# Softmax row sums of an attention and MoE kernel: probabilities added up per block on two engines, one ones product a block, eight shared PSUM banks

## The reference

```python
x = x + _layernorm(_L0_attn_ref(_layernorm(x), wq, wk_down, wv_down, wk_up, wv_up, wo))
x = x + _layernorm(_L0_ffn_ref(_layernorm(x), gate, experts, shared, anchors))
# attention: x is (2, 1024, 128), 8 heads in 2 groups, latent width 32
scores = jnp.einsum('bqhrd,bkhd->bhrqk', q, k) * scale
scores = jnp.where(causal, scores, jnp.finfo(scores.dtype).min)
probs = jax.nn.softmax(scores, axis=-1)
y = jnp.einsum('bhrqk,bkhd->bqhrd', probs, v)
```

## Time and profile before

| | us |
|---|---|
| median of 3 runs | 416.88 |
| lowest, highest | 416.11, 418.38 |
| the profiled execution's own time | 416.28 |
| its span, from the first to the last instruction | 414.2 |
| TensorE matmuls busy | 393.9 (95%) |
| VectorE busy | 281.5 (68%) |
| GpSimd busy | 275.7 (67%) |
| ScalarE busy | 231.4 (56%) |
| mean granted TensorE clock | 0.986 |

### The profile page before, as it was taken

How to read it: one execution, slowest core, us unless ns; L and a number is a source line. 1 busy time by engine, 2 the same in 40 slices (tenths; PEclk the granted TensorE clock), 3 DMA queues, 4 the chain that set the end, 5 groups by cost and what they waited for, 6 DMA issues and landing times.

```text
span 414.2 us, 7003 instructions
## 1 busy us (share of the span) xinstructions
PE 393.9 (95%) x2168; PEld 260.5 (63%) x2168; DVE 281.5 (68%) x711; ACT 231.4 (56%) x450; POOL 275.7 (67%) x338
## 2 busy tenths in 40 slices
PE   8998999998999999999998999999999999999993
PEld 8664555553454644444556778767887788778871
DVE  5985897882857885526347776678765686557665
ACT  4555355564545466664675455865556655665643
POOL 6124867975976498473667886498963988477651
PEclk9989999998999999999999999999999999999997
DMA  7347090083230050500000000001000000000000
GB/s 215 52 108 169 16 220 13 0 196 52 40 38 3 2 77 3 71 9 2 3 0 2 1 1 2 0 0 28 1 1 2 25 2 0 1 2 25 0 2 25
DMA packets 9906, 14.56 MB, mean 35 GB/s; under 512 B 1232, under 2 KB 5520, under 8 KB 9488
## 3 DMA queue, kind: packets, MB, share of 16 engines
q1 hardware_dynamic: 9584, 13.49, 15.7%
q10 hardware_dynamic: 288, 0.64, 0.5%
HBM read 6.26 MB, written 1.05 MB: 18 GB/s over the span
## 4 chain that ended last, share of the span: by engine, by line
PE 77%; POOL 7%; DVE 6%; ACT 4%; issue 3%; DMA 2%; SPq 1%; POOLq 0%; DVEq 0%; ACTq 0%
PE ps L1240 9%; PE ps L1242 9%; PE ps L1241 9%; PE ps L1354 9%; PE ps L1333 9%; PE acc L1368 8%; PE total L1378 5%; PE acc L1439 4%; PE acc L1441 4%; PE acc L1440 4%; POOL silu L839 3%; DMA qst<-q_lo 2%; PE ps L1336 2%; PE ps L1356 1%; PE ps L1388 1%
## 5 line engine op out<-in xcount | busy, mean ns | idle before, releaser
L839 POOL TENSOR_TENSOR silu<-silu,cwb 128x512 f32<-128x512 f32 x80 | 102.5, 1292 | 40.3 <-ACT silu L971 35.8
L1095 DVE TENSOR_REDUCE nmax_h<-ps 128x1 f32<-128x512 f32 (+3 forms) x152 | 92.3, 655 | 47.8 <-PE ps L1336 24.3
L940 ACT ACTIVATE probs<-ps 128x512 f32<-128x512 f32 (+1 forms) x152 | 80.0, 579 | 70.2 <-PE ps L1354 43.7
L759 POOL TENSOR_TENSOR probs<-probs 128x768 f32<-128x768 f32 (+2 forms) x48 | 78.0, 1644 | 34.0 <-ACT probs L940 21.2
L1172 DVE TENSOR_TENSOR h_lo<-ps,h_hi 128x512 fp32r<-128x512 f32 (+1 forms) x84 | 57.0, 686 | 23.8 <-ACT h_hi L981 23.2
L1167 DVE TENSOR_TENSOR ps<-silu,ps 128x512 f32<-128x512 f32 (+1 forms) x84 | 57.9, 693 | 22.3 <-POOL silu L839 17.5
L971 ACT ACTIVATE silu<-ps 128x512 f32<-128x512 f32 x80 | 47.5, 597 | 45.5 <-PE ps L1242 39.7
L1333 PE MATMUL ps<-kst,qst 96*128 96x512 f32 (+3 forms) x192 | 63.8, 386 | 4.0 <-ACT probs L940 1.9
L1240 PE MATMUL ps<-xT_hi,w_hi 128*128 128x512 f32 x164 | 65.4, 399 | 1.3 <-ACT silu L971 1.3
L1242 PE MATMUL ps<-xT_hi,w_lo 128*128 128x512 f32 x164 | 64.4, 393 | 0.0
L1241 PE MATMUL ps<-xT_lo,w_hi 128*128 128x512 f32 x164 | 64.4, 393 | 0.0
(11 more groups left out here) (191 smaller groups left out, 518.7 us busy)
## 6 DMA issues: line engine op xcount, KB each, us to landing
qst<-q_hi SPq DMA_DIRECT2D x14, 256.0 KB, 5.6
qst<-q_lo SPq DMA_DIRECT2D x7, 256.0 KB, 6.1
x_sb<-in_attn_x SPq DMA_DIRECT2D x4, 256.0 KB, 6.5
raw<-in_ffn_w_gate SPq DMA_DIRECT2D x1, 1024.0 KB, 4.9
raw<-in_ffn_w_up SPq DMA_DIRECT2D x1, 1024.0 KB, 6.4
raw<-in_ffn_w_down SPq DMA_DIRECT2D x1, 1024.0 KB, 5.0
kst<-k_hi SPq DMA_DIRECT2D x6, 128.0 KB, 3.7
result<-x_sb SPq DMA_DIRECT2D x3, 256.0 KB, 2.3
```

The lines of the kernel that those rows point to most:

```text
L759: nc.gpsimd.tensor_tensor(into, into, probs[:, k % KTBUF, js, cols], ALU.add).then_inc(added, 1)
L839: nc.gpsimd.tensor_tensor(silu[:, k % HRING, :], silu[:, k % HRING, :], cwb[:, m % 2, t // ET, :], ALU.mult).then_inc(scaled_ready, 1)
L940: nc.scalar.activation(probs[:, k % KTBUF, j:j + w, at:at + cols], bank(full)[:, 0:w * cols].rearrange("p (w c) -> p w c", w=w), ACT.Exp). ...
L1095: nc.vector.tensor_reduce(nmax_h[:, n % 2, i, j:j + w, h], bank(full)[:, 0:w * keys].rearrange("p (w k) -> p w k", w=w), AX.X, ALU.max, ne ...
```

## The change

The sums of a block are now all gathered in the buffer of its first tile, the others being added to it one after the other. Each later tile is added by two instructions: GpSimd takes the first `SPLIT[n]` heads of block n, VectorE the rest. The split is 2 and 2 in blocks 0, 6 and 7, and 3 and 1 in blocks 1 to 5. The ones product is made once a block. The first tile's buffer stays taken until this product is made, so three buffers turn for the other tiles (`buffers()`); an `exp` waits for both adds of the tile that lay there before. `acc` and `total` are gone as named banks: `pv`, `ones`, `down`, the warming products and the tail take their banks from one pool of eight. The first `silu`, `hi` and `lo` wait only for the buffer that each lies over (`rows_left`), not for the whole second pass.

```diff
-BANKS = 6
+BANKS = 8
+ADDERS = ("POOL", "DVE")
+SPLIT = (2, 3, 3, 3, 3, 3, 2, 2)
...
+def part_heads(n, part):
+
+    return (SPLIT[n], REP) if part else (0, SPLIT[n])
...
-                if kt % 2:
-                    for half in range(2):
-                        step("POOL", ("add", n, kt, half), 2 * (8 + cols * 252 // 1000), rank - 0.1, ("pv", n, kt - 1),
-                             *[e for e in exps if half in halves_of(e)])
-                    step("PE", ("ones", n, kt - 1), 10 + (CH - first_col(n, kt - 1)) * 17 // 100, rank - 0.2, ("add", n, kt, 0), ("add", n, kt, 1),
-                     ("ones", n, kt - 3) if kt > 1 else n >= 1 and ("recip", n - 1))
+                for part, engine in enumerate(ADDERS):
+                    if kt:
+                        j, end = part_heads(n, part)
+                        cost = 18 + (end - j) * cols * 215 // 1000 if engine == "POOL" else 15 + (end - j) * cols * 105 // 1000
+                        step(engine, ("add", n, kt, part), cost, rank - 0.1, ("pv", n, 0), *[e for e in exps if part in parts_of(e)], kt > 1 and ("add", n, kt - 1, part))
+        step("PE", ("ones", n), 10 + CH * 17 // 100, n + 2.9, *(("add", n, kts(n) - 1, part) for part in range(len(ADDERS))), bank=1, until=("recip", n))
...
+                elif kind == "add":
+                    _, n, kt, part = ev
+                    j, end = part_heads(n, part)
+                    cols = slice(first_col(n, kt), CH)
+                    into = probs[:, BUF[n, 0], j:end, cols]
+                    dve.wait_ge(pv_done, PV["pv", n, 0])
+                    dve.wait_ge(exp_ready, max(EXP["exp", *e[1:]] for e in p2_steps(n) if e[2] == kt and part in parts_of(e)))
+                    if kt > 1:
+                        dve.wait_ge(added[part], ADD[part]["add", n, kt - 1, part])
+                    nc.vector.tensor_tensor(into, into, probs[:, BUF[n, kt], j:end, cols], ALU.add).then_inc(added[part], 1)
...
-                        if okt % 2:
-                            act.wait_ge(added, ADD["add", on, okt, 1])
+                        if okt == 0:
+                            act.wait_ge(ones_done, ONES["ones", on])
                         else:
-                            act.wait_ge(ones_done, ONES["ones", on, okt])
+                            for part in range(len(ADDERS)):
+                                act.wait_ge(added[part], ADD[part]["add", on, okt, part])
...
-                    if k == 0:
-                        act.wait_ge(pv_done, len(PV))
-                        act.wait_ge(ones_done, len(ONES))
                     if k >= HRING:
                         act.wait_ge(h_ready, H["h", k - HRING])
+                    else:
+                        rows_left(act, k)
```

More of the change, by code:

```diff
@@ L208, in chunk_of, with leaves @@
         return CPB * b + c
+    def leaves(user, parts=range(len(ADDERS))):
+        if user is None:
+            return []
+        n, kt = user
+        return [("pv", n, kt), *(("add", n, kt, part) for part in parts)] if kt else [("ones", n)]
     step("SP", ("x_load",), 320, 0)
@@ L390, in plan @@
     return o, o.settle()
[L393 to L394 removed]
+BUF, WAS = buffers()
 PLACED, PLAN = plan()
@@ L541, in tiles, with sums, rows_left @@
             return ap.rearrange("p (t d) -> p t d", d=D)
+        def sums(m):
+            return bank(("down", MT * m))
+        def rows_left(engine, row):
+            kt = (1, 2, 3, 0)[row // REP]
+            engine.wait_ge(pv_done, PV["pv", NB - 1, kt])
+            for part in range(len(ADDERS)):
+                engine.wait_ge(added[part], ADD[part]["add", NB - 1, kt, part])
         def tail_tiles(half):
-            return tiles((total if half else bank(("tail_T", 0)))[:, 0:CH // 2])
+            return tiles(bank(("tail_T", half))[:, 0:CH // 2])
         def normed_of(ev):
@@ L592, in build @@
         pv_done = sem("pv_done")
-        added = sem("added")
+        added = [sem(f"added{part}") for part in range(len(ADDERS))]
         ones_done = sem("ones_done")
```

140 lines of the change are left out of this document (75 added, 65 removed).

## The result

The changed kernel takes 440.14 us in the median of 4 runs (435.94 to 440.84), the kernel before 416.5 us on the same chip; the ratio is 1.054, with a 95% interval from 1.047 to 1.062. It is slower, as the likeliest case said, but by 23.6 us in place of 3.5, and above the range. The profiled execution took 439.83 us with a span of 437.8.

What follows compares the result with a forecast made beforehand. TensorE was taken as the bound everywhere; after the change VectorE would be last in 42 to 165 us. +6.5 there and -3.0 behind make +3.5 us on the profiled span, hence 420.4 us; range 406 to 434.

Steps and rivals of the forecast that it cites:

- the likeliest case: Whole kernel: VectorE becomes last and the time rises to 420.4 us; with its surroundings, 415 to 427, chance 0.45.
- the relief of TensorE: Ones products fall from 24 to 8, taking 12.7 us off TensorE; time 404 if TensorE stays the bound.
- GpSimd and VectorE, alone: Work of the adds without waits: 94.7 us on GpSimd against 78.1 before, 23.6 us new on VectorE.
- What the adds wait for: VectorE's two-operand adds wait for GpSimd's running instruction: 1.5 us a full tile, 24.3 us in 42 to 165 us.
- One sign: VectorE's adds of 512 columns would end within 0.1 us of the end of a GpSimd instruction.
- The sum: 42 to 165 us takes VectorE's need, 129.5 us, 6.5 more; 3.0 us gained behind it; +3.5 us in all.
- (d): TensorE's granted clock falls when it stands: 5% on 30 us, 1.5 us added; chance 0.20 together with (c).
- the term of -3.0 us: Behind 165 us VectorE has room, so 3.0 us of TensorE's 4.3 us relief there remain as gain.
- the banks "at nothing": The edits to the banks cost nothing, since `pv` waited only 0.5 us in all for its bank.
- (a): TensorE stays last, VectorE's waits falling into gaps or idle time: 404 to 413 us; chance 0.35 together with (b).
- (b): GpSimd's add chain with three turning buffers is last: about 409 us; chance 0.35 together with (a).
- (c): VectorE arrives right behind GpSimd's start: 2.9 us a full tile, 438 us; chance 0.20 together with (d).

Runs made afterwards that it cites:

- e4_banks: The kernel before, with all products taking banks from one pool of eight; its pairwise GpSimd adds and 24 ones products stay; 407.14 us, ratio 0.972.
- e1_reduce: The changed kernel with VectorE's 40 adds made one-operand reductions into scratch, so its share is missing from the row sums; 405.19 us, ratio 0.969.
- e6_longer: e1_reduce with most of VectorE's reductions repeated two or three times, holding it for some 52 us; 416.87 us, ratio 0.996.
- e13_nm_reduce: The changed kernel with the subtraction of `nm_split` made a reduction over zeros, so the low half of the maxima is left out; 431.63 us, ratio 1.036.
- e11_longest: e1_reduce with VectorE's reductions repeated two to four times, about 68 us of them intended; 429.56 us, ratio 1.025.
- e3_pool_only: The changed kernel with both adds of each tile on GpSimd, two heads each, none on VectorE, and the order planned anew; 441.91 us, ratio 1.055.
- e16_reduce_seven: e1_reduce with seven banks in the pool in place of eight; 419.71 us, ratio 1.007.
- e7_true_cost: The changed kernel with VectorE's adds entered in the planner at their traced durations, giving all engines other fixed orders; 461.71 us, ratio 1.106.

## Why the prediction was wrong, and where it was right

**What bounds the kernel, and the relief of TensorE.** The pages were read rightly: TensorE was the last, and the ones products shrank as said (21.9 us in the group before, 10.3 after). But 12.7 us taken from its queue left about 2 us in net, with eight banks and no waiting add (e4_banks and e1_reduce); the forecast of 404 for this case is near e1_reduce's 405.2, but by luck, since the bank brought most of it.

**GpSimd and VectorE, alone.** 94.7 us was forecast for GpSimd's adds, 96.8 measured, of which a part is GpSimd's own waiting (94.4 in e6_longer, where VectorE has no adds). 23.6 us was forecast for VectorE's work alone; reductions over the same columns took 23.2 in e1_reduce.

**What the adds wait for.** Right in mechanism and size: four long blocks at 8.3 us of waits and four short ones at 1.6 make 23.6 + 39.6 = 63.2 us by the prediction's prices, 64.9 measured; the stretch's 42 to 165 us show VectorE 94% busy and TensorE idle for 16.6 us, its waits ended by maxima, as listed. (Two thirds of block 4's 8.3 us are 5.5 and not the 4.5 of the sum, a slip that matters little.) One sign was stated wrongly: the adds of 512 columns don't end within 0.1 us of a GpSimd instruction but 0.55 us behind it, since their own work comes after the wait. Missed was that `nm_split`, whose waits the prediction used as its evidence, would wait as well: 6.5 us more, worth 8.5 in e13_nm_reduce.

**The sum.** This step failed, in three of its terms. First, it set the time of the stretch equal to VectorE's need, 129.5 us, as if two engines that wait for each other could be used fully. GpSimd's last add of block 4 ended at 168.36 us before and at 184.42 after, 16.1 us late where 6.5 were forecast; a part of this is clock, see (d). Second, the term of -3.0 us behind 165 us had the wrong sign. VectorE's room there (28 us) was taken for slack, but it was not: block 5's last add ended 24.3 us late (214.9 against 190.6), 8.3 more than block 4's, and from 165 to 217 us TensorE stood for 6.9 us where it had stood for 0.6, at a clock of 0.80 and 0.85. e11_longest shows without a single waiting add what both terms left out: VectorE held for 45 us more than in e1_reduce costs 24 us and makes TensorE stand for 39.2 us in place of 22.5, though VectorE isn't full in either stretch (118.6 of 123 and 48.3 of 52 us). Third, the banks "at nothing", argued from the 0.5 us for which `pv` waited, measured about -10 us in e4_banks, with the new order that goes with them. The wait of `pv` was the wrong row for them: it shows 0.5 us; that the gain comes from the scores, which can take the bank that idles, is argued and not shown.

**The rivals.** (a) TensorE last and (b) GpSimd last did not happen; e3_pool_only shows what (b) looks like. (c), 438 us, has nearly the right time and the wrong reason: the waits were not 2.9 us at a full tile (the adds of 512 columns took 2.2 us in the mean, 1.5 more than alone). (d), the clock, was the rival that took the time out of the range, and it was mis-sized: 1.5 us forecast as an addition, 17.5 in the books above. It was priced as 5% on one stretch of 30 us, but the stalls were to come in all blocks, and the row with 0.93 at 88% busy was a warning of what a TensorE with stalls can get. Its own sign, a clock row below 0.9, is there at 0.80 and 0.85.

Without (d) the sum would have come near: TensorE's 18.8 us of new idle time less the 12.7 of relief are +6.1, beside +3.5. That closeness is partly luck, since it holds the -10 us of the bank.

**What stays open.** What pattern of standing lowers the clock. e11_longest stands as long as the changed kernel in sum and kept 0.974; e16_reduce_seven stands far less (24.1 us) and had 0.947. The idle sum doesn't tell it, and each profile is one execution. Nor is all added busy time surely clock: from e1_reduce to e11_longest it grew by 8.9 us, while the time not granted, estimated as above, grew by only 4.3. Also open is the bad order of e7_true_cost.

**The best version** of these that computes everything is e4_banks at 407.1 us: 2.8% below the kernel before and 7.5% below the changed one.

## What to carry to other kernels

Before a VectorE instruction is added beside a busy GpSimd, look at its form: with two SBUF operands, or as a plain multiplication from SBUF to SBUF, it lasts until GpSimd's running instruction ends, and so do the small ones of this form that are there already; a reduction doesn't, nor did an instruction with one operand from PSUM (`h_lo`, 512 columns: 0.656 to 0.693 us in all 84 instances of the kernel before). If a change makes TensorE stand in short pieces, price its clock first, from rows of the same kernel, over all stretches in which it will stand, and give the price a wide range: 92% busy went with 0.88 in e16_reduce_seven, 87% with 0.96 in e11_longest. A buffer that is held by one owner is priced by who could use it while it idles, not by how long the owner waits for it.
